# Starting an attention before its last keys and queries are moved, with a softmax bound for half of the queries

## The reference, cut to what matters

```python
xn = layernorm(layernorm(x), ln_gamma, ln_beta)
q, k, v = (heads(xn @ w.T) for w in (w_q, w_k, w_v))       # 4 heads of 64, 2048 tokens
qn = rmsnorm(q, q_gamma) * 64 ** -0.5
kn = rmsnorm(k, k_gamma)
attn = softmax(qn @ kn.T)                                   # over the 2048 keys
out = merge(attn @ v) @ w_o.T + b_o
x = x + layernorm(out)
chosen = argmax(x @ gate_w.T)                               # one of 8 experts a token
x = x + layernorm(x + expert_w[chosen] @ x)
```

## Time and profile before

| | us |
|---|---|
| three runs | 770.95, 779.7, 772.59 |
| median | 772.59 |
| profiled execution | 768.41 |
| its span | 766.6 |
| TensorE busy | 657.3 (86%) |
| VectorE busy | 597.1 (78%) |
| ScalarE busy | 540.8 (71%) |
| GpSimd busy | 270.2 (35%) |

### The profile page before, as it was taken

The page is one execution under the profiler, slowest core; times in us unless marked ns, Lnnn a source line. Parts: engine busy times, 40 slices in busy tenths (PEclk is TensorE's granted clock), DMA queues, the critical chain, the costliest instruction groups (busy, mean ns, idle before and its releaser), DMA issues.

```text
span 766.6 us, 21998 instructions
## 1 busy us (share of the span) xinstructions
PE 657.3 (86%) x8908; PEld 446.4 (58%) x8908; DVE 597.1 (78%) x1137; ACT 540.8 (71%) x870; POOL 270.2 (35%) x454
## 2 busy tenths in 40 slices
PE   4988859999999999868899699999999998705882
PEld 2666644666666666756667436666566567605772
DVE  4899965878877888896987658888887888963984
ACT  3377878888888888581777788888888785712552
POOL 2246664232332322000655532323233220071775
PEclk9699979999999999995998889999999999956997
DMA  7910007897979888120000078888798881024551
GB/s 250 274 33 1 1 1 143 154 161 140 166 142 163 154 148 145 57 83 29 29 29 29 29 136 154 155 150 160 142 166 150 149 152 57 2 96 134 171 168 43
DMA packets 53815, 87.13 MB, mean 114 GB/s; under 512 B 6608, under 2 KB 23250, under 8 KB 53460
## 3 DMA queue, kind: packets, MB, share of 16 engines
q0 software_dynamic: 34848, 65.61, 44.6%
q1 hardware_dynamic: 18020, 18.03, 8.1%
q10 hardware_dynamic: 848, 2.10, 0.8%
HBM read 14.82 MB, written 14.79 MB: 39 GB/s over the span
## 4 chain that ended last, share of the span: by engine, by line
PE 50%; DVE 21%; DMA 11%; ACT 8%; issue 8%; POOL 1%; SPq 0%; POOLq 0%; DVEq 0%; ACTq 0%
PE banks L1227 14%; PE banks L1086 11%; DMA e_h<-e_f 7%; PE banks L1245 6%; PE banks L1246 5%; DVE e_l L880 5%; PE banks L1247 5%; PE banks L1138 4%; ACT e_f L573 2%; DMA e_x<-x_all 2%; DVE x_all L925 1%; PE banks L1327 1%; DVE e_l L795 1%; PE banks L1141 1%; PE banks L1158 1%
## 5 line engine op out<-in xcount | busy, mean ns | idle before, releaser
L880 DVE TENSOR_TENSOR e_l<-e_f,e_h 128x1024 f16<-128x1024 f32 x172 | 206.2, 1222 | 58.4 <-DMA e_h<-e_f 51.9
L573 ACT ACTIVATE e_f<-banks,nbias,c_ 128x1024 f32<-128x1024 f32 x172 | 198.8, 1201 | 44.2 <-PE banks L1227 42.7
L1227 PE MATMUL banks<-q_T,k_T 128*128 128x512 f16 (+1 forms) x1024 | 204.4, 385 | 3.8 <-ACT nm L562 1.4
L1247 PE MATMUL banks<-v_mm,e_l 128*128 128x65 f16 x2048 | 201.6, 191 | 0.0
L1247 PEld LDWEIGHTS banks<-v_mm,e_l 128*128 128x128 f16 x2048 | 189.6, 99 | 0.0
L1245 PEld LDWEIGHTS banks<-v_mm,e_h 128*128 128x128 f16 x1376 | 126.0, 96 | 44.9 <-issue 23.7
L1245 PE MATMUL banks<-v_mm,e_h 128*128 128x65 f16 x1376 | 136.7, 193 | 9.1 <-DVE e_l L880 4.6
L407 POOL DMA_DIRECT2D e_h<-e_f x146 | 77.4, 530 | 179.3 <-ACT e_f L573 174.6
L1246 PE MATMUL banks<-v_mm,e_h 128*128 128x64 f16 x1376 | 136.1, 195 | 0.0
L1246 PEld LDWEIGHTS banks<-v_mm,e_h 128*128 128x128 f16 x1376 | 127.2, 97 | 0.0
L880 DVE TENSOR_TENSOR e_l<-x_all,e_x 128x1024 f16<-128x1024 f32 x84 | 101.1, 1222 | 20.8 <-DMA e_x<-x_all 17.9
(11 more groups left out here) (260 smaller groups left out, 1226.6 us busy)
## 6 DMA issues: line engine op xcount, KB each, us to landing
e_h<-e_f POOLq DMA_DIRECT2D x146, 256.0 KB, 3.9
e_x<-x_all POOLq DMA_DIRECT2D x72, 256.0 KB, 4.0
x_all<-x SPq DMA_DIRECT2D x12, 512.0 KB, 4.5
rows_d<-e_x SPq DMA_DIRECT2D x1, 5180.0 KB, 23.4
k_T<-rows_d SPq DMA_DIRECT2D x20, 259.0 KB, 3.2
attn_x<-weT ACTq DMA_DIRECT2D x1, 2048.0 KB, 7.8
q_T<-wqkvT SPq DMA_DIRECT2D x1, 768.0 KB, 6.2
out<-k_T POOLq DMA_INDIRECT x40, 2.6
```

Source lines behind the costliest of these rows:

```text
L573: act.activation(whole[s % NEF], ps_S[s % ALL % 3], ACT.Exp, bias=bias_of(h), scale=CESC).then_inc(s_E, 1)
L880: dve.tensor_tensor(low[s % NLO], whole[s % NEF], high[s % NHI], ALU.subtract).then_inc(s_El, 1)
L1227: ins = pe.matmul(ps_S[s % ALL % 3][:, c * BANK:(c + 1) * BANK], k_T[rows, 1 - c if cross else c, h * N + j * P:h * N + (j + 1) * P], q_T[ ...
L1247: ins = pe.matmul(o, low[s % NLO][:, at], v[:, 0:DH + 1], start=False, stop=j == NT - 1, skip_group_check=True)
```

## The change

The bound is formed apart for each half of the queries, from that half's `qn2` (`largest`, `largest_T`, `largest_diagonal`, `largest_everywhere`, `bias`). That of the first half (tiles 0 to 7) is formed inside the projection loop, spread over its last five tiles; its root is ScalarE's, `root_of_largest`, in tile 13. That of the second half is formed during the first steps of the attention; its root is VectorE's, from a guess by the exponent bits and two Newton steps, since ScalarE has the exponential's table by then. The exponential uses the bias of its half.

TensorE issues the scores of steps 0 and 1 before it transposes tile 14, those of step 2 before tile 15, then those of steps 3, 4 and 5, and the weighted sums of steps 0 and 1 ahead of scores 6 and 7. ScalarE loads the table right after the loop and places `high_qk` of tile 15 and the k moves of tiles 14 and 15 between exponentials 0, 1 and 2. VectorE moves q of tiles 14 and 15. The expert weights of the last three halves are written after exponentials 5, 6 and 7 by ScalarE and ahead of casts 8 to 10 by GpSimd. Slot numbers of the attention's buffers start anew with each batch. Leading blanks are cut and empty lines left out.

```diff
-    if b == 0:
-        for w in range(NT - 3, NT):
-            low_expert(w)
     for s in range(b * ALL, (b + 1) * ALL):
+        if 8 <= s < 11:
+            low_expert(NT - 11 + s)
+        if s == b * ALL + 2:
+            pool.wait_ge(s_T2, b * NT + NT - 1)
+        if s == b * ALL + 3:
+            pool.wait_ge(s_qs, b * NT + NT)
         if dma_casts(s):
...
-            pool.dma_start(high[s % NHI], whole[s % NEF]).then_inc(s_cast[s % NHI], 16)
...
+    def root_of_largest():
+        act.wait_ge(s_mxB, b * NQB + 1)
+        act.activation(top[:, :], ps_mB[0], ACT.Sqrt).then_inc(s_mx, 1)
...
-            if b == 0 and n >= 2:
+            if b == 0 and 2 <= n < NT - 1:
                 high_expert(n - 2)
             if t == 2 and not last:
                 high_y(g + 1)
             if not (first and t < 2):
                 move_k(n - 2, at - 2)
                 move_q(n - 2, at - 2)
+            if t == 1 and last:
+                root_of_largest()
...
-    high_qk(end - 1, NT - 1)
-    for t in range(NT - 2, NT):
-        move_k(b * NT + t, t)
-        move_q(b * NT + t, t)
-    if b == 0:
-        for w in range(NT - 2, NT):
-            high_expert(w)
-    act.wait_ge(s_mxB, b + 1)
-    act.activation(nm[:, 0:H], bank(0)[:, 0:H], ACT.Sqrt).then_inc(s_mx, 1)
-    if 2 * b > 0:
-        act.wait_ge(s_warm, 2 * b)
-    act.activation(warm[:, :], ones[:, 0:1], ACT.Exp).then_inc(s_warm, 1)
-    act.wait_ge(s_nb, 2 * b + 2)
     def exp_step(hh, h, k):
         s = hh * STEPS + k
+        if s == b * ALL + 1:
+            act.wait_ge(s_ss, end)
+        if s == b * ALL or s == b * ALL + NT:
+            act.wait_ge(s_nb, 2 * (b * NQB + k // NT) + 2)
         act.wait_ge(s_S, s + 1)
         if s - NEF + 1 > 0:
             act.wait_ge(s_El, s - NEF + 1)
+        act.activation(whole[s % ALL % NEF], ps_S[s % ALL % 3], ACT.Exp, bias=bias_of(h, k // NT), scale=CESC).then_inc(s_E, 1)
...
     def head_act(b, h):
         hh = b * H + h
         for k in range(STEPS):
             exp_step(hh, h, k)
+            if h == 0 and k == 0:
+                high_qk(end - 1, NT - 1)
+                move_k(end - 2, NT - 2)
+            if h == 0 and k == 1:
+                move_k(end - 1, NT - 1)
+            if b == 0 and h == 0 and k in (5, 6, 7):
+                high_expert(NT - 8 + k)
+    act.activation(warm[:, :], ones[:, 0:1], ACT.Exp).then_inc(s_warm, 1)
...
+            if gi == NG - 2 and t == 3:
+                largest(0)
+            if last and t == 0:
+                largest_diagonal(0)
+            if last and t == 2:
+                bias(0)
+    def largest(qb):
+        c, half = b * NQB + qb, QT * (qb + 1)
+        dve.wait_ge(s_qs, b * NT + half)
+        dve.tensor_reduce(qmx[:, :], qn2[:, half - QT:half, :].rearrange("p t h -> p h t"), AX.X, ALU.max).then_inc(s_mxD, 1)
+    def largest_diagonal(qb):
+        c = b * NQB + qb
+        dve.wait_ge(s_mxT, c + 1)
+        dve.tensor_reduce(qmT[:, :], ps_mT[qb], AX.X, ALU.max).then_inc(s_mxD, 1)
+        dve.wait_ge(s_mxD, 3 * c + 2)
+        dve.tensor_scalar(qmD[:, :], ident[0:H, 0:H], qmT[:, 0:1], None, ALU.mult).then_inc(s_mxD, 1)
+    def largest_out(qb):
+        c = b * NQB + qb
+        dve.wait_ge(s_mxB, c + 1)
+        dve.tensor_copy(top[:, :], ps_mB[qb]).then_inc(s_root, 1)
+    def root_of_largest(qb):
+        dve.wait_ge(s_root, 9 * b + 1)
+        dve.tensor_scalar(root2[:, :].bitcast(u32), top[:, :].bitcast(u32), 0.5, 532487680.0, ALU.mult, ALU.add).then_inc(s_root, 1)
+        for i in range(2):
+            dve.wait_ge(s_root, 9 * b + 2 + 4 * i)
+            dve.reciprocal(quot[:, :], root2[:, :]).then_inc(s_root, 1)
+            dve.wait_ge(s_root, 9 * b + 3 + 4 * i)
+            dve.tensor_tensor(quot[:, :], quot[:, :], top[:, :], ALU.mult).then_inc(s_root, 1)
+            dve.wait_ge(s_root, 9 * b + 4 + 4 * i)
+            dve.tensor_tensor(root2[:, :], root2[:, :], quot[:, :], ALU.add).then_inc(s_root, 1)
+            if i == 0:
+                dve.wait_ge(s_root, 9 * b + 5)
+                dve.tensor_scalar(root2[:, :], root2[:, :], 0.5, None, ALU.mult).then_inc(s_root, 1)
+    def bias(qb):
+        c = b * NQB + qb
+        if qb == 0:
+            dve.wait_ge(s_mx, b + 1)
+            dve.tensor_scalar(nbias[:, 0, :], top[:, :], -KSCALE * math.sqrt(DH), None, ALU.mult).then_inc(s_nb, 1)
+        else:
+            dve.wait_ge(s_root, 9 * b + 9)
+            dve.tensor_scalar(nbias[:, 1, :], root2[:, :], -KSCALE * math.sqrt(DH) / 2, None, ALU.mult).then_inc(s_nb, 1)
+        dve.wait_ge(s_nb, 2 * c + 1)
+        dve.tensor_scalar(nbias[:, qb, :], nbias[:, qb, :], CESC, TOP, ALU.mult, ALU.add).then_inc(s_nb, 1)
+    def move_q(n, at):
+        dve.wait_ge(s_T2, n + 1)
+        dve.tensor_copy(q_T[:, :].rearrange("p (h n) -> p h n", h=H)[:, :, at * P:(at + 1) * P],
...
-    if b == 0:
-        expert_mean(NT - 1)
-    dve.wait_ge(s_qs, b * NT + NT)
-    dve.tensor_reduce(qmx[:, :], qn2[:, :, :].rearrange("p t h -> p h t"), AX.X, ALU.max).then_inc(s_mxD, 1)
...
-    dve.wait_ge(s_nb, 2 * b + 1)
-    dve.tensor_scalar(nbias[:, :], nbias[:, :], -KSCALE * math.sqrt(DH), TOP, ALU.mult, ALU.add).then_inc(s_nb, 1)
+    move_q(end - 2, NT - 2)
+    largest(1)
+    move_q(end - 1, NT - 1)
+    largest_diagonal(1)
     def parts(hh, h, k):
         s = hh * STEPS + k
+        if s < b * ALL + 2:
+            dve.wait_ge(s_q2, end - 1 + k)
+            dve.wait_ge(s_hi, 2 * (end - 1 + k))
+        if s == b * ALL + 2:
+            dve.wait_ge(s_T2, end)
...
             parts(hh, h, k)
+            if h == 0 and k == 0:
+                largest_out(1)
+            if b == 0 and h == 0 and k == 2:
+                expert_mean(NT - 1)
+            if h == 0 and k == 4:
+                root_of_largest(1)
+                bias(1)
...
+            if last and t == 0:
+                largest_T(0)
+            if last and t == 1:
+                largest_everywhere(0)
+            if not (first and t < 1) and not (last and t == TG - 1):
                 transpose_qk(n - 1, t - 1)
...
+    def largest_T(qb):
+        c = b * NQB + qb
+        pe.wait_ge(s_mxD, 3 * c + 1)
+        pe.transpose(ps_mT[qb], qmx[:, :], ident[:, :]).then_inc(s_mxT, 1)
+    def largest_everywhere(qb):
+        c = b * NQB + qb
+        pe.wait_ge(s_mxD, 3 * c + 3)
+        pe.matmul(ps_mB[qb], ones[0:H, :], qmD[:, :], start=True, stop=True).then_inc(s_mxB, 1)
...
-    transpose_qk(b * NT + NT - 1, NT - 1)
-    pe.wait_ge(s_mxD, 3 * b + 1)
-    pe.transpose(bank(0)[0:H, 0:P], qmx[:, :], ident[:, :]).then_inc(s_mxT, 1)
-    pe.wait_ge(s_mxD, 3 * b + 3)
-    pe.matmul(bank(0)[:, 0:H], ones[0:H, :], qmD[:, :], start=True, stop=True).then_inc(s_mxB, 1)
-    pe.wait_ge(s_mx, b + 1)
-    pe.wait_ge(s_ke, b * NT + NT)
-    pe.wait_ge(s_qe, b * NT + NT)
...
     def head_pe(b, h):
         hh = b * H + h
-        for k in range(0, STEPS, 2):
-            scores(hh, h, k)
+        for k in range(0 if h else LAG, STEPS, 2):
+            scores(hh, h, k, k + 1)
             for i in (k - LAG, k - LAG + 1):
-                if i >= 0:
+                if i >= 2 or i >= 0 and h:
                     pv(hh, h, i)
                 elif h:
                     pv(hh - 1, h - 1, STEPS + i)
+    hh = b * H
+    pe.wait_ge(s_ke, end - 3)
+    pe.wait_ge(s_qe, end - 3)
+    pe.wait_ge(s_mx, b + 1)
+    scores(hh, 0, 0)
+    pe.wait_ge(s_qkn, end)
+    scores(hh, 0, 1)
+    transpose_qk(end - 2, NT - 2)
+    pe.wait_ge(s_vl, end)
+    pe.wait_ge(s_vh, 2 * end)
+    scores(hh, 0, 2)
+    transpose_qk(end - 1, NT - 1)
+    scores(hh, 0, 3)
+    pe.wait_ge(s_qe, end)
+    largest_T(1)
+    scores(hh, 0, 4, 5)
+    largest_everywhere(1)
+    pe.wait_ge(s_ke, end)
+    pe.wait_ge(s_root, 9 * b + 1)
+    pv(hh, 0, 0)
+    pv(hh, 0, 1)
```

46 lines of the change are left out of this document (23 added, 23 removed).

## The result

The changed kernel took **764.89 us** (median of 20 runs, 760.36 to 767.22), the kernel before 771.23 beside it (20 runs); the ratio is 0.9928 with a 95% interval of 0.9911 to 0.9945, so 5.6 us less (the two medians by themselves are 6.3 apart). That is "within 1%", the class with the chance of 0.89, but 5.6 us under the forecast point and 1.6 under the range. Part of that distance is not the change's: the forecast stood on a median before of 772.59, from three runs, and that median is 771.23 here. A gain of 2.0 from there would be 769.2, and the measured time lies 4.3 under it. The profiled execution took 765.08 (span 763.4), 3.3 less than that of before.

A forecast was written before the change was run, and what follows sets the result against it. TensorE was taken as the bound from the first weighted sum on, so only the stretch ahead could be won: 0.9 in batch 0 plus 1.1 in batch 1, 2.0 us, median 770.5 from 772.59; range 766.5 to 775.

The forecast's parts named there:

- within 1%: Outcome class for the whole kernel: no change beyond 1% (7.7 us), chance 0.89; faster 0.05, slower 0.06.
- Part 1: Projection loop: added VectorE work 1.3 and ScalarE's root 0.5 all count, so tile 15's normal q and k come 1.8 later.
- Parts 2 to 5: Start of attention, batch 0: exp 0 7.3 earlier, lead shrinking to 3.1, 2.5, 1.1, then 0.9 at steps 14 and 15.
- The q move: VectorE's move of q from PSUM at the seam: between 0.35 and 0.7 us, taken as 0.6.
- Parts 2 to 4: Batch 0: exp 0 at 109.2, exp 2 at 115.6, weighted sum 0 at 119.2, 4.0 earlier; lead 2.5 after scores 6 and 7.
- the root's row: VectorE behind step 4: ten small operations at pitch 0.25, 2.5 us, making its split of step 7 late.
- one cast is some 0.6 late, six steps ahead of its use: nothing: GpSimd in batch 0: expert halves ahead of casts 8 to 10 delay one cast by 0.6 us, costing nothing.
- The clock: TensorE at the seam: low (half-rate) clock assumed from 107 to 117 us; called the forecast's weakest point.
- Rival 1: Clock holds full rate through the seam; 1.3 and 1.5 more won in the batches, 4.8 in all, 767.8 us; chance 0.2.
- the rule that transposes do not count as activity: TensorE's clock at the seam: by this rule the low clock comes and the gain stays 2.0 us.
- Rival 2: Gaps of 0.5 to 0.8 at first weighted sums lower the clock at 117 to 120; 1.4 slower, 774.0 us; chance 0.18.
- Rival 3: VectorE's 2.5 and more added work before splits 5 to 8 makes TensorE wait; lead gone by step 8, 772.6; chance 0.17.

The follow-up runs named there:

- sums_after_6_7: Changed kernel with the scores of steps 6 and 7 ahead of weighted sums 0 and 1, as before; 764.55 us, ratio 0.9936 to the kernel before.
- root_sums: Changed kernel with second root and bias operations two at a time behind splits 3 to 7, scores 6 and 7 ahead of weighted sums 0 and 1; ratio 0.988.
- half_bound_only: Changed kernel with exponentials, transposes and moves of tiles 14 and 15 in the old order; 775.42 us, ratio 1.0073 to the kernel before.
- all_three: Changed kernel with scores 6 and 7 first, root operations strewn behind splits 3 to 7, GpSimd halves of tiles 14 and 15 one operation per cast; ratio 0.9951.
- root_late: Changed kernel with VectorE's root and bias of the second half behind step 10 instead of step 4; 768.38 us, ratio 0.9971 to the kernel before.
- change_again: The changed kernel, unedited, run again in the second comparison; 763.14 us, ratio 0.9914 to the kernel before.
- fill: Changed kernel plus 13 unread TensorE products, 5 behind step 0's scores and 8 behind step 2's; 781.38 us, ratio 0.9928 to the kernel before.
- comparisons 1 and 2: First two of four groups of runs, each beside the unchanged kernel before on its own chip: 769.58 and 770.08 us; the third and fourth 785.92 and 786.32.

## Why the prediction was wrong in size and right in shape

**Part 1 is the step that failed**: "all counts: 1.3 with the gaps of semaphores" and 0.5 for the root, "1.8 later". It measured 0.14 and 0.24, and loop_added, the kernel before with the same additions to its loop, has 0.14 and 0.23. I had read VectorE busy 3.60 of 4 us and called the rest "waits inside its own relay", hence no slack. But VectorE's wait for nr, four times 0.36, ends when ScalarE's own queue comes to nr, 0.5 after VectorE's sums are ready, so work put ahead of the sums is free up to there. ScalarE's root in turn stood in a time when it waited for TensorE anyway (it waited 2.5 in all for projected tiles in the loop before; now 1.8, and 0.4 for the root's product). Put right, the sum is 2.0 + 1.66 + 1.56 = 5.2, beside 5.6 measured and 6.1 in the profile: this step is 3.2 of the 3.6 us by which the gain was forecast too small. (Its last addition is off by a tenth: 766.4 and the difference of 4.2 make 770.6 and not 770.5.)

**Parts 2 to 5**, counted from the forecast start of tile 15's normal q and k (107.3 and 434.9 are its end, 0.69 later than its start), with the change's three executions:

| us after q15 | forecast, batch 0 | measured | forecast, batch 1 | measured |
|---|---|---|---|---|
| exp 0 | 2.6 | 2.33 | 2.7 | 2.33 |
| exp 2 | 9.0 | 8.00 to 8.01 | 9.0 | 8.25 to 8.38 |
| weighted sum 0 | 12.6 | 11.0 to 11.8 | 12.7 | 11.4 |
| split of step 7 ends | 24.0 | 25.1 to 25.2 | 23.8 | 22.5 to 22.7 |
| scores of step 14, in batch 1 of step 12 | 26.4 | 25.90 to 25.96 | 22.8 | 21.5 |

The order of waits came as said: tile 15's transposes wait for the q move, weighted sum 0 for the copy of the bound. The q move took 0.42, within 0.35 to 0.7 and under the 0.6 taken. Parts 2 to 4 were too dear by up to 1.3 us at weighted sum 0 in batch 1 and by 0.8 to 1.6 in batch 0, and the root's row, whose ten operations took 2.0 in batch 1 (pitch 0.20) and not 2.5, was too dear as well.

In batch 1 this stayed to the end: counted from q15 and less the loop's 0.24, the lead at the scores of step 12 is 3.9, beside a corrected forecast of 1.1 + 1.56 = 2.66. Some of that 1.3 may be the kernel before, whose batch 1 was up to 1.1 earlier at exp 12 in other executions (25.97 for 27.06).

In batch 0 the scores of step 14 came within 0.5 of the forecast, and that is luck. That "one cast is some 0.6 late, six steps ahead of its use: nothing" was wrong: the cast of step 10 came 3.2 late, VectorE's splits were slowed, and without GpSimd's halves the scores of step 14 come 1.7 earlier (low_experts_out; 1.2 is left at exp 24). What had been counted too dear made up for what had been left out.

**The clock** was taken at half rate from 107 to 117; in batch 0 it was so for 4 us or not at all, in batch 1 for 3 to 7 us. Rival 1's condition thus held in batch 0 of two executions. Its price for the transposes was right (0.5 forecast, 0.6 measured at exp 2, see "The clock" above). For the whole stretch it took 1.3 and 1.5. The shorter stretches of the change cost 0.6 to 0.8 at exp 8; where scores 6 and 7 stand first, batch 1 has exp 8 at 15.20 with no half rate (sums_after_6_7) and at 16.85 with some 10 us of it (root_sums), 1.65 later, of which 0.9 is left at exp 24. As for the rule that transposes do not count as activity (the Trainium skill, "TensorE: Matmul & The Clock Gate", Part 4): in the new kernel the clock stays at 1.00 from 104 to 114, with TensorE busy for 5.33 of these 10 us on three rounds of transposes and the scores of four steps, and in two other executions to 120, so the rule did not decide this case; the earlier trace rows at 110 to 112 is the one row that went with it.

**Rival 2**: in the changed kernel no fall of the clock after the first sums (1.00 from 118 to 150). It exists, though: in half_bound_only, all_three and root_late the clock went to 0.50 for some 3 us during or shortly behind rests of TensorE (1.24, 1.91 and 2.18). It does not follow every such rest: TensorE waited 1.48 for a split in change_again and 2.71 in fill, and the clock stayed. **Rival 3**: half there. TensorE did wait for a split (0.62 at 128.52, 1.48 in change_again), but the root's row alone is not the cause: in batch 1 it costs nothing.

**GpSimd and VectorE.** I had not asked what GpSimd's operations cost beside VectorE's splits. In the changed kernel a four-column operation of VectorE (L872) took 0.93, from 123.45 to 124.38, and 0.16 in batch 1; GpSimd's addition ran from 123.71 to 124.34 beside it. Without GpSimd's halves (low_experts_out) it took 0.16 in batch 0 too. The Trainium skill, "SBUF — State Buffer", Who interferes with whom, has the rule: the port pair that both share is an exclusive lock, and a VectorE operation with two SBUF inputs contends with a GpSimd operation that reads SBUF. A tensor-scalar operation, it says, can hold both ports too. The trace agrees: L872, begun 0.26 before GpSimd's addition, ended 0.04 after it, and GpSimd's subtractions took 1.59 and 1.60 for 0.73 beside splits. That the lock is the mechanism is by the page; no run here tells it from another kind of slowing.

## What to carry to other kernels

A wait inside a relay can be slack for work put ahead of it: it is where the other engine is busy with its own queue when its input is ready (here 0.5 us a tile), and not where that engine stands waiting for this one. Before an addition is charged in full, look at both, and charge what exceeds the slack. Count a forecast from an event near the change and not from the clock of the execution; here 1.6 us of shift from untouched stages looked exactly like a term of the sum. Parts of a reordering are not additive (expert weights: nothing alone, over 3 us in the new order), so undo each from the whole as well as doing it alone.

## What the runs showed of the hardware that was not expected

- GpSimd's 128x256 operations took 0.63 and 0.73 alone and up to 1.53 and 1.66 beside VectorE's splits; splits of 1.22 took up to 2.21, operations on four columns 0.16 or up to 0.93.
- TensorE's half rate falls differently from execution to execution of one program: 114 to 118, or not at all from 104 to 120, with exp 8 of batch 0 at 18.08 or 17.27. Twelve transposes of 128x128 took 0.83 at full rate and 1.44 at half, and what waited for them came 0.6 later.
- The same kernel differs by 2% between chips (769.58 and 786.32 for the one before). Nearly all of it lies behind the attention of batch 1: from the last exponential to the end the profiles of comparisons 1 and 2 take 130 to 133 us, those of 3 and 4 145 to 150.
